# GNN edge loop: two scans one pair earlier, the difference behind them one pair earlier

## The reference

```python
e = (edge_attr @ We).reshape(-1, H, C)
kj = k[src] + e
vj = v[src] + e
logits = jnp.einsum('ehc,ehc->eh', q[dst], kj) / np.sqrt(C)
m = jax.lax.stop_gradient(jax.ops.segment_max(logits, dst, num_segments=n))
ex = jnp.exp(logits - m[dst])
denom = jax.ops.segment_sum(ex, dst, num_segments=n)
a = ex / (denom[dst] + 1e-16)
agg = jax.ops.segment_sum(vj * a[:, :, None], dst, num_segments=n)
```

## Time and profile before

| | us |
|---|---|
| median of 3 runs | 4731.94 |
| lowest and highest | 4719.11, 4738.05 |
| profiled execution | 4729.83 |
| span in the profile | 4728.0 |

### The profile page before, as it was taken

One profiled execution on the slowest core, in us unless ns is written; L12 is line 12 of the kernel. 1 busy time (PEld: TensorE's weight loads), 2 busy tenths in 40 slices (PEclk: granted clock), 3 DMA queues, 4 the chain that ended last, 5 costly groups with the idle time before them and its releaser, 6 DMA issues. The chain is left out here.

```text
span 4728.0 us, 104277 instructions
## 1 busy us (share of the span) xinstructions
PE 4242.0 (90%) x19602; PEld 3462.7 (73%) x19603; DVE 3712.6 (79%) x8323; ACT 2969.8 (63%) x10407; POOL 2788.6 (59%) x2804
## 2 busy tenths in 40 slices
PE   7979999999999999979899999999999999649994
PEld 4557777777777777746677777777777777449993
DVE  5549998899899899955499998998998998644443
ACT  2217777777777777741167777777777777634331
POOL 1037777677677777700277776776776777244465
PEclk9989999999999999989999999999999999769997
DMA  5557777777777777725587776776777777342344
GB/s 130 163 159 220 209 207 205 201 206 207 203 205 206 206 207 206 205 91 163 167 233 207 208 211 195 209 209 199 208 210 205 208 209 202 111 165 89 98 137 123
DMA packets 577383, 874.82 MB, mean 185 GB/s; under 512 B 110389, under 2 KB 442229, under 8 KB 576598
## 3 DMA queue, kind: packets, MB, share of 16 engines
q0 software_dynamic: 150656, 488.11, 35.7%
q1 hardware_dynamic: 383536, 331.31, 24.3%
q10 hardware_dynamic: 42534, 48.33, 3.2%
HBM read 782.54 MB, written 84.87 MB: 183 GB/s over the span
## 5 line engine op out<-in xcount | busy, mean ns | idle before, releaser
L958 POOL DMA_INDIRECT edge_kv<-kvD,edge_ix x1760 | 1762.5, 1001 | 948.4 <-issue 471.8
L1005 ACT ACTIVATE edge_w<-edge_vj,edge_ex 128x64 f32<-128x64 f32 x7040 | 1864.2, 338 | 470.6 <-PE edge_pa L1046 297.7
L1023 PE MATMUL edge_ps<-edge_We,edge_ea 112*128 112x256 f32 x7040 | 1865.4, 387 | 51.9 <-DVE edge_prod L1158 22.8
L1023 PEld LDWEIGHTS edge_ps<-edge_We,edge_ea 112*128 112x128 f32 x7040 | 1341.4, 193 | 302.0 <-issue 64.9
L1046 PE MATMUL edge_pa<-edge_w,edge_oh 128*128 128x260 f32 x3520 | 1110.1, 398 | 95.9 <-DVE acc L1080 55.3
L1027 PE MATMUL edge_ps<-acc,edge_oht 128*128 x3520 | 1068.5, 385 | 0.5 <-issue 0.5
L1046 PEld LDWEIGHTS edge_pa<-edge_w,edge_oh 128*128 128x128 f32 x3520 | 635.3, 192 | 289.2 <-issue 117.9
L1080 DVE TENSOR_TENSOR acc<-acc,edge_pa 128x260 f32 x1760 | 736.6, 419 | 118.3 <-PE edge_pa L1046 63.4
L1126 DVE TENSOR_TENSOR edge_kj<-edge_kv,edge_ps 128x512 f32<-128x512 f32 x880 | 601.9, 684 | 254.6 <-PE edge_ps L1027 141.9
L1027 PEld LDWEIGHTS edge_ps<-acc,edge_oht 128*128 128x128 f32 x3520 | 682.5, 194 | 99.3 <-issue 1.2
L1158 DVE TENSOR_TENSOR edge_prod<-edge_kj,edge_ps 128x512 f32<-128x512 f32 x880 | 601.0, 683 | 0.0
(11 more groups left out here) (265 smaller groups left out, 3804.5 us busy)
## 6 DMA issues: line engine op xcount, KB each, us to landing
edge_ea<-ea_t_dram SPq DMA_DIRECT2D x1760, 112.0 KB
edge_kb<-relD SPq DMA_DIRECT2D x178, 160.0 KB
edge_kv<-kvD,edge_ix POOLq DMA_INDIRECT x1760
ffn_xr<-xsD SPq DMA_DIRECT2D x112, 128.0 KB
ysD<-ffn_yo SPq DMA_DIRECT2D x112, 128.0 KB
kvD<-open_kvs ACTq DMA_DIRECT2D x49, 256.0 KB
kvD<-mid_kvs ACTq DMA_DIRECT2D x49, 256.0 KB
edge_pen<-penD SPq DMA_DIRECT2D x352, 32.0 KB
```

Of the source, the lines that this page charges most:

```text
L958: nc.gpsimd.indirect_dma_start(out=kv[:, j % HT, :], out_offset=None, in_=g.kvD, in_offset=bass.IndirectOffsetOnAxis(ap=ix[:, h, j % HT:j ...
L1005: nc.scalar.activation(w[:, j % 4, h * CA:h * CA + C], vj[:, slot, h * C:(h + 1) * C], ACT.Copy, scale=ex[:, x, h, k:k + 1])
L1023: nc.tensor.matmul(ps[:, j % 4, 0:D], ea[:, j % HT, k, :], We[:, k, :], start=(k == 0), stop=(k == 1))
```

## The change

It moves five VectorE instructions of the once-a-chunk chain one pair earlier and alters none of them. The two scans over 128 columns, F2 and B2, go from pair q = 4 to pair q = 3, at the same places within the pair (behind `prod` and behind the reduction). The difference `Df` with `dl`, and `Ym`, go from pair q = 5 to pair q = 4, again at the same places (behind `kj` and behind `vj`). Pair q = 5 then has no extra work. No wait is added or removed, and no other engine's list changes.

```diff
-                    if q == 5 and closed(c):
+                    if q == 4 and closed(c):
                         step(11)
                         nc.vector.tensor_tensor(Df[:, :], MT, B2[:, :], ALU.subtract).then_inc(s_D, 1)
                         nc.vector.scalar_tensor_tensor(out=dl[:, :], in0=GX[:, 15:16], scalar=B2[:, 0:1], in1=B2[:, 0:1],
...
-                    if q == 5 and closed(c):
+                    if q == 4 and closed(c):
                         step(12)
                         nc.vector.tensor_scalar(Ym[:, :], mask4[:, :], dl[:, 0:1], None, ALU.mult).then_inc(s_Y, 1)
...
-                    if q == 4 and closed(c):
+                    if q == 3 and closed(c):
                         step(8)
                         nc.vector.tensor_tensor_scan(F2[:, :], pen[:, o, 0, :], MT, GX[:, 15:16], ALU.add, ALU.max).then_inc(s_m, 1)
...
-                    if q == 4 and closed(c):
+                    if q == 3 and closed(c):
                         step(10)
                         nc.vector.tensor_tensor_scan(B2[:, rev], pen[:, o, 1, rev], F2[:, rev], GY[:, 16:17], ALU.add, ALU.max).then_inc(s_m, 1)
```

## The result

The changed kernel takes 4743.59 us (median of 18 runs, 4737.61 to 4752.93) beside 4735.33 us for the kernel before (18 runs): ratio 1.0021, 95% interval 1.0012 to 1.003. I had forecast 4647. Its profiled execution has a span of 4742.6 us at a granted clock of 0.963, where before had 0.956.

The account below looks back on a forecast made before the run. PE and VectorE were taken to hold each other up, with at most some 270 us of the edge loops recoverable. From 4729.8 us, minus 55 for the wait and 32 for the clock, plus 4, came 4647; range 4575 to 4745.

Parts of the forecast that it names:

- The bound and the wait: Edge loops: at most some 270 us to regain; PE's transposition waits for `Df` in 71 of 88 chunks, 1.94 us in one.
- The slip: PE's steps 10 to 12 wait for VectorE's moved work; step 12 starts 1.03 us late in all.
- `Df` and `dl` at 0.33: VectorE, pair q = 4: the two moved instructions together take 0.33 us of its line, as in their old place.
- the 1.3 that I had named as a sign of being wrong: PE before step 12: new idle time above 1.3 us would show the prediction wrong.
- The late count: PE's count of step 11 reaches VectorE's `kj` of q = 5 over 3 us late, unexplained.
- Cases A and B: `kj` of q = 5: count late as before, 4647 us, chance 0.40; or count in time, 4590 us, chance 0.27.
- The clock: PE's granted clock in the edge loops rises from 0.98, giving back 32 us, or 50 with the count in time.
- E: Rival: the count, and so `kj` of q = 5, comes later by the whole slip; 4716 us, chance 0.17.
- D: Rival: short idle pieces in each chunk pull PE's clock to half there as well; 4791 us, chance 0.08.
- C: Rival: step 11's count is released only when PE has nothing to run; 4771 us, chance 0.08.

Follow-up runs that it names:

- e6: The changed kernel with only step 18's GpSimd zero copy, the one that meets `dl`, issued behind its gather, on chip B: 4549.75 us, ratio 1.0158.
- f3: The changed kernel with only step 18's GpSimd zero copy issued behind its gather, on chip C: 4661.47 us, ratio 0.9864 to the kernel before.
- f1: The changed kernel as it stands, run again beside the kernel before on chip C: 4740.06 us, ratio 1.0022.
- h1: The kernel before with each GpSimd zero copy cut in two, so at most two gathers follow each other: 4608.70 us, ratio 0.9762.
- i2: The kernel before with each GpSimd zero copy cut into four, one ahead of every gather: 4616.95 us, ratio 0.9757.
- h2: The kernel before with GpSimd's gathers running 8 steps ahead in place of 10: 4829.29 us, ratio 1.0220.
- e5b: The kernel before with one 128x1 `scalar_tensor_tensor` added beside the copy, one input in PSUM, on chip B: 4483.82 us, one execution.

## Why the prediction was wrong

- **The bound and the wait: right.** The wait for `Df` is gone, and steps 13 to 15 won 2.6 us a chunk, 2.0 without the clock, where I had counted 1.03 + 0.78 = 1.8.
- **The slip: right in itself.** 1.2 us at steps 11 and 12 in e6, with `dl` free, against 1.03.
- **`Df` and `dl` at 0.33: the step that failed.** I took durations from the old place to the new. `dl` is struck by the copy in 80 chunks, 1.24 us more each, 99 us. So step 12 lost 2.0 us in the median where I had 1.03, past the 1.3 that I had named as a sign of being wrong. The rows of before put the two side by side. By my own slip the add of step 8 comes at 1019.44; `kj`, `Df` and `dl` follow 0.33, 0.60 and 0.20 us apart, so `dl` at 1020.57, and the copy runs from 1020.91 (GpSimd's lines above), 0.34 us behind, as 1027.43 is behind 1027.07 in the changed kernel. At 0.21 us `dl` would have ended 0.13 us ahead of the recorded start, so those rows give a near miss and not yet the collision; that an instruction is struck which began up to 0.62 us before that start is known only from the changed kernel. I had looked at GpSimd only for what its gathers wait for. The chunk of the earlier trace rows even has a struck B2. With one copy moved (f3) the change wins 67 of the forecast 83 us; with the copy where it is (f1, same chip), nothing: 79 us between them.
- **The late count: a wrong footing.** Cases A and B asked whether it moves. Neither asked if it is always there. It fell away in part by itself (3.7 to 0.4 us at step 11) and on chip B it doesn't exist, where the change, with `dl` free, is 70 us slower. Its own gain is thus a gain on the lateness.
- **The clock: about right and small.** 0.98 to 0.99 in the window; the time at half clock fell from 134 to 67 us over both loops, so 33 us came back where I had taken 32.
- **The rivals: none is what happened.** E (4716) came nearest in time but by another mechanism: `kj` didn't come later with the slip. `kj` of q = 5 follows its add at 1031.44 without idle time. D's half-clock stretches hardly came: steps 11 to 13 hold 23 us at half clock in both loops (1 before), where D, with 116 us lost, needs 233, and 102 are gone from steps 14 and 15.
- **The chances.** Those of A and B add up to 0.67, not 0.68, and C and D to 0.16.

What stays open: why PE's counts are held. That it goes with runs of gathers is borne out by h1, i2 and the releases; that the gathers cause it was not isolated, since no run takes the gathers away. Why chip B doesn't do it, with the same gathers in the same rhythm, isn't known, nor was the changed kernel as it stands timed there.

## What to carry to other kernels

Before you move an instruction, list what every other engine does in the new window, and look for an operand pair: two SBUF inputs on VectorE beside a GpSimd operation that reads SBUF cost the rest of that operation, whatever their own size. When a wait rests on something that you can't explain, find out what makes it before you pay to go around it: here the cheaper edit was on GpSimd, 2.4% against nothing. And repeat a close result on another chip; one of five ran the kernel before 5% faster, and the sign of this edit, with its collision removed, turned there (0.9864 on C, 1.0158 on B).

## What the runs showed of the hardware

- A scan over 20 columns with two SBUF inputs took 0.256 us in the median of before and 2.99 in h2, where GpSimd runs a tensor operation of 2.34 us and a copy of 1.06 there.
- `scalar_tensor_tensor` on 128x1 with both inputs in SBUF: 0.21 us alone, 0.86 and 1.45 us in the median beside a copy of 1.06 us by GpSimd, its end 23 ns behind the copy's; with one input in PSUM 0.208 us. The instruction of 1.45 us began 0.37 us (median) before the recorded start of the copy.
- Four chips agree on the kernel before within 0.05% (4727.01 to 4729.41 us). On the fifth it takes 4479.28. In e5b there, the edge loops' long operations (matmuls of L1023, L1027 and L1046, `kj`, `vj`, `prod`, the copy, the gathers) have the median durations of before within 1%, and the counts of steps 10 and 11 come 0.2 us behind the matmuls in place of 2 to 4 us.
- On the four, TensorE's counts come out in bunches, in before 0.43 to 1.08 us behind the end of GpSimd's last gather. In that trace the counts of VectorE and GpSimd come 10 to 11 ns behind the instruction's end (median).
